# Gated row, dot product and squares one attention slot back, statistics in two buffers

## What is computed

```
ada = t_emb @ w_ada + b_ada                    # sh, sc, g for attention; the same for the MLP
xn  = layer_norm(logmap0(x));  xm = expmap0(xn * (1 + sc_msa) + sh_msa)
q, k, v = _to_heads(plin(xm, w, b)) for the three weights    # 16 heads of 16
attn = softmax(qt @ kt.T / 4);  out_h = expmap0(attn @ vt)
attn_t = g_msa * logmap0(plin(_from_heads(out_h), w_o, b_o))
x = mobius_add(x, expmap0(attn_t))             # needs x.x, z.z, zg.zg, x.zg, sum(zg) of every token
```

## Time and profile before

| | |
|---|---|
| median of 3 runs | 842.89 us (840.26 to 843.83) |
| the profiled execution | 841.73 us, span 839.9 us |
| TensorE matmul busy | 703.7 us, 84% |
| VectorE busy | 673.6 us, 80% |
| ScalarE busy | 586.5 us, 70% |
| GpSimd busy | 353.3 us, 42% |

### The profile page before, as it was taken

The page is one execution under the profiler, slowest core; times in us unless marked ns, Lnnn a source line. Parts: engine busy times, 40 slices in busy tenths (PEclk is TensorE's granted clock), DMA queues, the critical chain, the costliest instruction groups (busy, mean ns, idle before and its releaser), DMA issues.

```text
span 839.9 us, 29703 instructions
## 1 busy us (share of the span) xinstructions
PE 703.7 (84%) x9393; PEld 515.0 (61%) x9393; DVE 673.6 (80%) x2231; ACT 586.5 (70%) x1627; POOL 353.3 (42%) x682
## 2 busy tenths in 40 slices
PE   5967999999999999999999999731868899889986
PEld 2756777777777777777777777520325555556555
DVE  3868888888888888888888888757797888888885
ACT  1125777777777777777777777633577888888874
POOL 1005555556555565555555565401232333233231
PEclk9979999999999999999999999955899999999999
DMA  9931111111111111111111110021343545455432
GB/s 324 354 86 52 51 52 51 56 56 46 50 54 56 56 43 51 56 56 52 44 54 56 55 46 27 23 66 51 88 116 98 148 137 144 126 150 151 138 102 100
DMA packets 51811, 73.99 MB, mean 88 GB/s; under 512 B 7081, under 2 KB 34609, under 8 KB 51762
## 3 DMA queue, kind: packets, MB, share of 16 engines
q1 hardware_dynamic: 49970, 70.55, 28.4%
q10 hardware_dynamic: 1792, 2.89, 0.9%
HBM read 64.24 MB, written 9.18 MB: 87 GB/s over the span
## 4 chain that ended last, share of the span: by engine, by line
PE 44%; DVE 25%; issue 14%; DMA 5%; ACT 4%; SPq 3%; DVEq 2%; POOL 2%; POOLq 0%; ACTq 0%
PE p_qkv L893 21%; PE p_oz L867 8%; DVE u L1156 7%; PE p_s L958 3%; PE p_s L883 3%; DMA mod_b<-mod_rows 3%; SPq L365 2%; DVE g_all L1191 2%; PE p_qkv L958 2%; PE p_oz L861 2%; DMA x_all<-in_x 2%; DVEq L50 2%; PE p_t L944 1%; DVE qk L1231 1%; PE p_o L972 1%
## 5 line engine op out<-in xcount | busy, mean ns | idle before, releaser
L893 PE MATMUL p_qkv<-wqkv,tT 128*128 128x256 f32 x768 | 194.3, 390 | 26.6 <-DVE u L1156 26.3
L893 PEld LDWEIGHTS p_qkv<-wqkv,tT 128*128 128x128 f32 x768 | 135.1, 192 | 57.4 <-issue 23.8
L477 POOL TENSOR_TENSOR qk<-qk 128x512 f16<-128x512 f32 x64 | 73.9, 1155 | 142.0 <-ACT qk L613 142.0
L907 PEld LDWEIGHTS p_o<-v,pT 64*64 64x64 f32 x4096 | 68.3, 136 | 36.1 <-issue 36.1
L1184 DVE TENSOR_TENSOR z<-p_oz,bo 128x256 f32<-128x256 f32 x64 | 27.1, 424 | 77.5 <-PE p_oz L867 77.3
L618 ACT ACTIVATE qkT<-p_s 128x1024 f32<-128x1024 f32 x64 | 65.5, 1023 | 31.1 <-PE p_s L850 31.1
L907 PE MATMUL p_o<-v,pT 64*64 64x17 f32 x4096 | 72.8, 209 | 12.0 <-ACT pT L663 12.0
L663 ACT ACTIVATE pT<-p_s 128x1024 f32<-128x1024 f32 x64 | 65.4, 1022 | 20.3 <-PE p_s L883 20.3
L867 PE MATMUL p_oz<-wo,oT 128*128 128x256 f32 x256 | 75.2, 418 | 0.6 <-ACT oT L623 0.5
L850 PE MATMUL p_s<-ident,qk 128*128 128x128 f16 x1024 | 67.9, 219 | 6.7 <-issue 4.5
L1222 DVE TENSOR_TENSOR qk<-u,fac 128x256 f32<-128x256 f32 x128 | 70.3, 588 | 0.1
(11 more groups left out here) (268 smaller groups left out, 1758.0 us busy)
## 6 DMA issues: line engine op xcount, KB each, us to landing
mod<-mod_rows SPq DMA_DIRECT2D x128, 128.0 KB, 2.8
x_all<-in_x SPq DMA_DIRECT2D x8, 1024.0 KB, 13.9
gate<-mod_rows SPq DMA_DIRECT2D x128, 64.0 KB, 2.5
mod<-mod_rows SPq DMA_DIRECT2D x32, 256.0 KB, 4.1
mod_b<-mod_rows SPq DMA_DIRECT2D x32, 256.0 KB, 4.1
out<-x_all SPq DMA_DIRECT2D x32, 256.0 KB, 2.2
gate<-gate_rows SPq DMA_DIRECT2D x32, 128.0 KB, 3.5
bqkv<-gate_rows SPq DMA_DIRECT2D x32, 128.0 KB, 3.8
```

Source lines behind the costliest of these rows:

```text
L477: pool.tensor_tensor(low, qk[:, :].rearrange("p (a h d) -> p a h d", a=2, d=HD), qk4[:, :, :, 0, :], ALU.subtract).then_inc(low_ready, 1)
L893: mm = pe.matmul(p_qkv[:, a * D:a * D + D], tT[:, k, c, :], wqkv[:, c, a * D:a * D + D], start=c == 0, stop=c == C - 1)
L907: mm = pe.matmul(p_o[S * e:S * e + S, col:col + VW], pT[keys, e, g, :], v[keys, k, 2 * g + e, :], start=True, stop=True, skip_group_check= ...
```

## The change

The gated row with its sum (`gate_z`), the dot product with x (`dot_x`) and the square of the gated row (`square_zg`, now a function of its own), with `keep_stats`, get a lag of their own, `L_G` = 7, one slot behind `add_bo`. On VectorE `gate_z`, `clip_t` and `dot_x` stand ahead of `add_bo` and `repeat_parts` in the second part of a slot, where they stood behind or between them. On ScalarE `square_zg` stands ahead of `square_z`. On POOL `token_root` moves ahead of `low_parts`. `st` has two buffers, and the waits for `stats_kept` ask for one copy less. All engines run one slot more at the end. SyncE's slot is the same as before.

```diff
--- before.py
+++ after.py
@@ -149,7 +149,7 @@
         o = sb("o", [P, TB, G, HD])
         oT = sb("oT", [P, 2, TB, S])
         z = sb("z", [P, D])
-        st = sb("st", [P, 4])
+        st = sb("st", [P, 2, 4])
         junk = sb("junk", [P, 4, D], BF16)
 
 
@@ -284,7 +284,7 @@
 
 
 
-        L_A, L_B, L_C, L_D, L_E, L_H, L_L = 0, 1, 2, 3, 4, 5, 6
+        L_A, L_B, L_C, L_D, L_E, L_H, L_L, L_G = 0, 1, 2, 3, 4, 5, 6, 7
         FIRST = 8
         M_A, M_Q, M_B, M_N, M_P, M_D, M_O = 0, 1, 2, 6, 7, 8, 9
         TURN = 8
@@ -323,7 +323,7 @@
             return min(n, T) if isinstance(n, int) else n
 
         def run_tiles(eng, slot):
-            run_slots(eng, slot, FIRST, T, T + L_L)
+            run_slots(eng, slot, FIRST, T, T + L_G)
 
         def run_pairs(eng, slot):
             for s in range(HALF + M_O):
@@ -477,22 +477,23 @@
                 pool.tensor_tensor(low, qk[:, :].rearrange("p (a h d) -> p a h d", a=2, d=HD), qk4[:, :, :, 0, :],
                                    ALU.subtract).then_inc(low_ready, 1)
 
-            def keep_stats(i):
+            def keep_stats(i, k):
                 pool.wait_ge(z_squared, i + 1)
                 pool.wait_ge(zg_squared, i + 1)
                 pool.wait_ge(xg_summed, i + 1)
-                pool.tensor_copy(stats[:, bass.ds(i, 1), :].rearrange("p a n -> p (a n)"), st[:, :]).then_inc(stats_kept, 1)
+                pool.tensor_copy(stats[:, bass.ds(i, 1), :].rearrange("p a n -> p (a n)"), st[:, k, :]).then_inc(stats_kept, 1)
 
             def slot(h, off):
                 if on(h, off, L_E):
                     scale_v(2 * h + off - L_E, (off - L_E) % 2)
-                    low_parts(2 * h + off - L_E)
                 if on(h, off, L_C):
                     token_root(2 * h + off - L_C, (off - L_C) % 2)
+                if on(h, off, L_E):
+                    low_parts(2 * h + off - L_E)
                 if on(h, off, L_D):
                     head_roots(2 * h + off - L_D)
-                if on(h, off, L_L):
-                    keep_stats(2 * h + off - L_L)
+                if on(h, off, L_G):
+                    keep_stats(2 * h + off - L_G, (off - L_G) % 2)
 
             run_tiles(pool, slot)
 
@@ -647,15 +648,17 @@
                 after(act, roots_ready, i)
                 act.activation(y0[:, :], lnh[:, :], ACT.Exp, scale=-0.5).then_inc(y0_ready, 1)
 
-            def square_z(i):
+            def square_z(i, k):
                 act.wait_ge(z_ready, i + 1)
-                after(act, stats_kept, i)
+                after(act, stats_kept, i - 1)
                 after(act, z_squared, i)
-                act.activation(junk[:, 1, :], z[:, :], ACT.Square, accum_out=st[:, 0:1]).then_inc(z_squared, 1)
+                act.activation(junk[:, 1, :], z[:, :], ACT.Square, accum_out=st[:, k, 0:1]).then_inc(z_squared, 1)
+
+            def square_zg(i, k):
                 act.wait_ge(zg_ready, i + 1)
                 after(act, zg_squared, i)
                 act.activation(junk[:, 2, :], g_all[:, bass.ds(i, 1), :].rearrange("p a d -> p (a d)"),
-                               ACT.Square, accum_out=st[:, 3:4]).then_inc(zg_squared, 1)
+                               ACT.Square, accum_out=st[:, k, 3:4]).then_inc(zg_squared, 1)
 
             def exp_scores(i):
                 act.wait_ge(s_psum, i + 1)
@@ -680,8 +683,10 @@
                     inverse_norms(2 * h + off - L_D)
                 if on(h, off, L_A):
                     square_t(2 * h + off - L_A, (off - L_A) % 2)
+                if on(h, off, L_G):
+                    square_zg(2 * h + off - L_G, (off - L_G) % 2)
                 if on(h, off, L_L):
-                    square_z(2 * h + off - L_L)
+                    square_z(2 * h + off - L_L, (off - L_L) % 2)
 
             run_tiles(act, slot)
 
@@ -1187,16 +1192,16 @@
 
                 dve.wait_ge(z_ready, i + 1)
                 dve.wait_ge(gate_in[k], 32 * half + 32)
-                after(dve, stats_kept, i)
+                after(dve, stats_kept, i - 1)
                 dve.scalar_tensor_tensor(out=tile_of(g_all, i), in0=z[:, :], scalar=1.0, in1=gate[:, k, :],
-                                         op0=ALU.mult, op1=ALU.mult, accum_out=st[:, 1:2]).then_inc(zg_ready, 1)
-
-            def dot_x(i):
+                                         op0=ALU.mult, op1=ALU.mult, accum_out=st[:, k, 1:2]).then_inc(zg_ready, 1)
+
+            def dot_x(i, k):
 
                 dve.wait_ge(zg_ready, i + 1)
                 after(dve, xg_summed, i)
                 dve.scalar_tensor_tensor(out=junk[:, 3, :], in0=tile_of(x_all, i), scalar=1.0, in1=tile_of(g_all, i),
-                                         op0=ALU.mult, op1=ALU.mult, accum_out=st[:, 2:3]).then_inc(xg_summed, 1)
+                                         op0=ALU.mult, op1=ALU.mult, accum_out=st[:, k, 2:3]).then_inc(xg_summed, 1)
 
             def limit(i):
 
@@ -1254,20 +1259,20 @@
                     sum_rows(2 * h + off - L_D)
 
             def slot_from_bias(h, off):
+                if on(h, off, L_G):
+                    gate_z(2 * h + off - L_G, (off - L_G) % 2, h + (off - L_G) // 2)
+                if on(h, off, L_C):
+                    clip_t(2 * h + off - L_C, (off - L_C) % 2)
+                if on(h, off, L_G):
+                    dot_x(2 * h + off - L_G, (off - L_G) % 2)
                 if on(h, off, L_L):
                     add_bo(2 * h + off - L_L)
                 if on(h, off, L_E):
                     repeat_parts(2 * h + off - L_E)
-                if on(h, off, L_L):
-                    gate_z(2 * h + off - L_L, (off - L_L) % 2, h + (off - L_L) // 2)
-                if on(h, off, L_C):
-                    clip_t(2 * h + off - L_C, (off - L_C) % 2)
-                if on(h, off, L_L):
-                    dot_x(2 * h + off - L_L)
                 if isinstance(h, int) and 2 * h + off == T + 3:
                     split_ff_bias()
 
-            run_slots_rotated(dve, slot_until_rows, slot_from_bias, FIRST, T, T + L_L)
+            run_slots_rotated(dve, slot_until_rows, slot_from_bias, FIRST, T, T + L_G)
```

## The result

The changed kernel takes 869.38 us (median; 868.58 to 870.99), the kernel before 843.36 us beside it: ratio 1.032 (95% interval 1.029 to 1.035), 26 us slower. The forecast was 856 us with a range of 838 to 864: the direction and the mechanism are the forecast ones, the size is twice the forecast one and outside the range.

A forecast was written before the change was run, and what follows sets the result against it. The prediction took a new ring through SyncE's wait for `gate_z` as the bound: 15.62 us for two slots, 7.81 against 7.55, times 56 = +14.6 us. With -1.5 for ramp and tail, about +13: 856 us, range 838 to 864.

The forecast's parts named there:

- the ring: From `gate_z` through SyncE's queue, `mod` and `modulate` to the next `gate_z`: 7.81 us a slot, above today's 7.55.
- the idle time of about 0.7 before `limit`: Sign expected in the profile after: VectorE idle about 0.7 us before `limit`, waiting for POOL.
- release of `gate_z` to `gate`, to second `mod`: On SyncE: `gate_z`'s read-out end to first `gate` issue 0.39 us, then to second `mod` issue 4.40, two slots.
- landing and VectorE's wake: `mod` issue to landing 5.70 us, then landing to `modulate` 0.40, for two slots.
- `modulate` to `sum_rows`: On VectorE, start of `modulate` to start of `sum_rows`, running without a gap: 1.65 us, twice 3.30.
- `sum_rows` to `gate_z`: On VectorE, start of `sum_rows` to start of `gate_z`: 0.51 us for two slots, the loop's return included.
- `gate_z` to its read-out's end: On VectorE, start of `gate_z` to the end of its read-out: 0.92 us for two slots.
- The loop's return on VectorE: Delay before `gate_z` where the loop returns: up to 0.11 + 0.36 us, the 0.36 being SyncE's return cost.
- rival 1: Slack in the SyncE ring, which falls below 7.37 us a slot; the roots' ring bounds: 831 us, chance 0.12.
- the roots' ring: Scores, exponential, inverse norms, roots, `normalise`, TensorE's second projection: mean 7.37 us a slot, the next bound of the compute.
- The 0.90 us off the ring: `gate_z`, `clip_t`, `dot_x` leave the old `add_bo`-to-`project` ring, fitting VectorE's 1.14 us idle time before `add_bo`.
- Ramp and tail: Slots outside the loop's new ring, where the moved steps leave VectorE's path: -1.5 us (0 to -3).

The follow-up runs named there:

- f1: The changed kernel with SyncE issuing the gate rows one slot later (lag 6 for 5): 827.62 us, ratio 0.985.
- f3: The changed kernel with one more 1 KB DRAM-to-DRAM transfer issued by SyncE behind the two gate transfers of every slot: 932.72 us, ratio 1.110.
- f8: The kernel before with SyncE's wait ahead of the gate rows asking for one `gate_z` more (i for i - 1): 920.63 us, ratio 1.096.
- f9: f6 with SyncE's gate rows at lag 5, as in the kernels before and after: 816.29 us, ratio 0.974.
- f2: The changed kernel with POOL's fp16 low parts cut to one head, 16 columns in place of 512: 853.24 us, ratio 1.016.
- f6: f1 with VectorE's order changed: `gate_z` behind `modulate`, then `shift_t`, `dot_x`, and `sum_squares` moved last; full computation: 816.67 us, ratio 0.973.
- f5: f1 with POOL's low parts cut to one head as in f2: 812.28 us, ratio 0.968.
- f7: f1 with POOL's old order, `low_parts` ahead of `token_root`: 895.03 us, ratio 1.066.

## Why the prediction was right and wrong

**Right: the mechanism.** What bounds next is the ring `gate_z`, SyncE, `mod`, `modulate`, `gate_z`, read off the waits' counts and an untouched engine. f1, f3, f8 and f9 move the time the way that the ring's sum says: 42 us less without it, 63 more with one more issue, 80 more when closed in the old kernel, nothing when it is shorter than the slot. One of the prediction's signs mostly failed: the idle time of about 0.7 before `limit` came in 13 slots, 7.7 us in all.

**Wrong: two terms of the sum.** The two turns above took 7.77 + 8.42 = 16.19 us, against 15.62. By the prediction's own terms, the last column being twice the mean of the 45 turns between 120 and 480 us:

| term, two slots | predicted | these two turns | 45 turns |
|---|---|---|---|
| release of `gate_z` to `gate`, to second `mod` | 0.39 + 4.40 | 0.39 + 4.40 | 0.39 + 4.39 |
| landing and VectorE's wake | 5.70 + 0.40 | 3.14 + 3.08 = 6.22 | 6.13 |
| `modulate` to `sum_rows` | 3.30 | 1.87 + 1.71 = 3.58 | 3.61 |
| `sum_rows` to `gate_z` | 0.51 | 0.12 + 0.63 = 0.75 | 0.67 |
| `gate_z` to its read-out's end | 0.92 | 0.42 + 0.43 = 0.85 | 0.97 |
| sum | 15.62 | 16.19 | 16.17 |

The step that failed is the term `modulate` to `sum_rows`: it was taken as fixed, 1.65 a slot, "these run without a gap", and measured 1.81. There is no gap, but the operations grew: with VectorE late, `shift_t` came to lie beside POOL's `low_parts`, 468 ns in the kernel before and 614 on the mean after. Before, `low_parts` ran in VectorE's idle time ahead of `add_bo`. I filled that idle time in the sum without asking who else was using it. f2 prices the stretching, of `shift_t` and of `gate_z` (499 ns for 421) together, at 13 to 16 us of the loss.

The Trainium skill (GPSIMD Engine Reference, Specifications) says that GpSimd's SBUF interfaces are shared with VectorE, with contention for VectorE instructions that have two SBUF inputs. The measurements agree: `gate_z` and `shift_t`, with two such inputs, grow (0.42 to 1.30 us in f1, 468 to 614 ns in the kernel after); `sum_squares`, with one, doesn't (0.94 us in f6).

The loop's return on VectorE was the other one: 0.63 from `sum_rows` to `gate_z` where the loop returns, above my upper end of 0.47, which I had borrowed from SyncE's return. `issue` ahead of `gate_z` is 10.0 us over 25 slots.

**Right with another cause: rival 1.** The change without the ring came to 827.6 us against 831, but in f1 VectorE was the bound, full with the stretched `gate_z`; with that gone (f5, f6) the slot fell to 7.11 and 7.19, so the roots' ring is shorter than the 7.37 of the prediction. `head_roots`' own operations had been read at the length that they had in the old order: 402.03 to 404.27 in the kernel before, 2.24 us, against 2.17 on the mean of its loop and 1.78 in f6. The 0.90 us off the ring did not fit into VectorE's idle time either: `gate_z` alone takes 1035 ns there in f1.

**The range.** Its upper end was 8.0 a slot, with all unknown terms together at 8.1; the measured 8.13 needed the stretching, which no term had: without it (f2) the slot is 7.89 and the time, 853.2 us, within the range. That all terms at their high ends also give 8.1 is chance, since the landing and the wake stayed in the middle of theirs. (By the prediction's own terms its ends for two slots are 14.71 and 16.19, not 14.6 and 16.3, so its low end hardly reaches rival 1's 14.74.)

**Ramp and tail** gave 3 us against 1.5; TensorE's wait moved to the transposes behind the repeats (57.0 us), as said in general, not by name. The granted clock of 0.96 in the loop (1.00 before) was not forecast. The ring has no TensorE in it, and the terms above account for the slot without the clock: 16.17 for two.

## What to carry to other kernels

When a step is moved a stage back, list who waits for its semaphore, the transfer queues above all, and what stands behind that wait in the same queue: close the ring and sum it before counting the gain. Idle time of an engine is not free room: look at what the other engines run in it, since in these runs an operation of VectorE with two SBUF inputs, put beside a long one of GpSimd, took up to three times as long. A wait can be loosened by issuing the waiting transfer a slot later, or the ring shortened by moving the releasing step right behind the released one.

## What the runs showed that I had not expected

A two-input operation of VectorE that starts behind a long GpSimd instruction ends about when that does: 0.42 us becomes 1.30 beside 1.15 (f1). All 54 `gate_z` of f1's loop end 0.28 to 0.29 us behind the end of `low_parts`, and so do, at 0.28, the 47 operations stretched beyond 0.52 us beside it in the kernel after: they look held back until it ends rather than slowed. The granted TensorE clock was lower where TensorE waited longer for VectorE's repeats: 1.00 in f1 (28.7 us in 100 to 500), 0.96 in the kernel after (49.2), 0.91 in f7 (46.8) and 0.88 in f3 (66.3). The order isn't strict, and whether the lower clock cost time of its own was not separated in any run. One more small issue on SyncE costs 0.90 us between its neighbours, not the 0.67 of the others (f3).
